# Attention sums: GpSimd adds all four key tiles into two sets of buffers, TensorE sums once per group, the output bias moves to VectorE

## The chip, the cores and the metric

The kernel runs on one core of one Trainium2 chip. A core has five engines with a queue each: TensorE (PE in the profile; PEld is its weight load), VectorE (DVE), ScalarE (ACT), GpSimd (POOL) and SyncE (SP), which issues the DMAs here. They run side by side and meet at semaphores only. The metric is device time in microseconds (us) of one execution; lower is better.

## The reference, cut to what matters

Four layers run one after another over x (4 batches of 512 tokens, 512 channels): a scan layer, a quantized feed-forward layer, an attention layer, and a last quantized projection. The change is in the attention layer:

```python
q = q.reshape(B, N, H, Dh)            # H = 16 heads of Dh = 32; N = M = 512
attn = softmax(einsum('bnhd,bmhd->bhnm', q, k) * scale, axis=-1)
o = einsum('bhnm,bmhd->bnhd', attn, v).reshape(B, N, C)
out = _qdq(o) @ _qdq(wp).T + bp
```

The result is added to x with a factor tanh(g). The bias bp, times that factor, may be added to x at any time before that; the kernel does it row by row during the attention.

## The kernel before, in words

**Groups and slots.** The attention is 16 groups: 4 batches times 4 sets of 4 heads (`HG` = 4). A group is 16 slots: slot 4t + j handles key tile t (128 keys) and head j. TensorE's `attend` writes out what each slot issues, in this order: the row matmuls of the next group (`rows`, L1161, whose maxima VectorE takes), the slot's score matmul (`scores`, L1180: 128 keys by 512 queries), then what the slot has besides. ScalarE turns each score tile into weights with an exponential (L936) and stores it in one of eight buffers `PR`. There are two PSUM banks for scores, so the score of slot s waits for the exponential of slot s - 2. Once a key tile is through, `weigh` (L1190, four matmuls of f32, eight records) multiplies the weights with the values.

**The maxima and their transfer.** The softmax needs each query's maximum before the scores begin. The row matmuls of group n + 1 run in the slots of group n (`ROWS` says how many in each; three PSUM banks take turns, so a row matmul waits for the reduction three before it). VectorE reduces each one (`maxima`, L1641). After slot 9 TensorE turns the maxima (`c_turn`, L1169); ScalarE casts them to f16 behind the exponential of slot 10 (`c_out`, L909); VectorE makes the remainder in its slot 12 (`c_low`, L1649); SyncE sends both to the operand of the next group's scores (L447, two DMAs). The first score of the next group waits for them (`c_in`).

**The sums.** The softmax's denominator is a sum of the weights over all keys. For key tiles 0, 1 and 2 GpSimd adds the weights, one buffer `ACC[j]` per head (L663, eight adds a group). TensorE then sums over the partitions with a matrix of ones, into PSUM bank 7: in slot 2 of the following group the weights of tile 3 (`sum_last`, L1209), in slot 3 the `ACC` buffers (`sum_weights`, L1199). ScalarE copies the sums out of bank 7 (`sums_out`, L921) behind the exponential of slot 5. TensorE turns the sums in slot 6 (`sum_turn`, L1227, into bank 4) and the outputs in slot 7 (`o_turn`, L1217, into bank 7, so it waits for that copy). VectorE inverts the sums in slot 8 (L1655) and normalizes the outputs in slot 9 (L1661). After a group's adds GpSimd adds the bias to one row block of x (L666).

**What sets the order.** Every engine's order is written out by hand, slot by slot; an engine takes its instructions strictly in that order and waits at each for its semaphores.

The functions that the diff touches, with what calls them:

Of the kernel before, what the change touches and what calls it, by code (L numbers as in the profile page):

```python
# [5 lines left out]
F32 = mybir.dt.float32  # L6
# [54 lines left out]
def flamingo_kernel(nc, x, ctx_2048, g_xattn, g_ffn, w, u, w1, w2, w3, wq, bq, wkv, bkv, wp, bp, gamma, wl, out):  # L61
    stack = ExitStack()
    with stack:
# [124 lines left out]
        ACC = [part(SEQ, F32) for _ in range(HG)]  # L188
# [321 lines left out]
        def _(pool):  # L510
# [142 lines left out]
            def add_weights(b, first, last):  # L653
                for g in range(DB):
                    n = b * DB + g
                    for t in (1, 2):
                        for j in range(HG):
                            pool.wait_ge(exp_done, n * 16 + HG * t + j + 1)
                            if t == 1:
                                up_to(pool, sum_ps, n)  # L660
                            else:
                                pool.wait_ge(acc_done, n * 8 + j + 1)
                            nc.gpsimd.tensor_tensor(ACC[j], PR[j] if t == 1 else ACC[j], PR[(HG * t + j) % 8],  # L663
                                                    ALU.add).then_inc(acc_done, 1)
                    rows = X[:, bass.ds(n, 1), :].rearrange("p a d -> p (a d)")
                    nc.gpsimd.tensor_tensor(rows, rows, bp_all[:, :], ALU.add).then_inc(x_biased, 1)  # L666
# [22 lines left out]
        def _(act):  # L689
# [233 lines left out]
            def attend(b, first, last):  # L923
                for g in range(DB):
                    n = b * DB + g
                    opening, closing = first and g == 0, last and g == DB - 1
                    for t in range(TB):

                        up_to(act, pv_tile, n * TB + t - 1)
                        for j in range(HG):  # L930
                            if t == 1:
                                up_to(act, sum_ps, n)
                            else:
                                up_to(act, acc_done, n * 8 + (j - 3 if t == 0 else j + 1))
# [5 lines left out]
                            if (t, j) == (1, 1) and not opening:  # L940
                                sums_out(*preceding(b, g))
# [54 lines left out]
        def _(pe):  # L996
# [167 lines left out]
            def c_turn(b, g):  # L1164
                n = b * DB + g
                pe.wait_ge(row_max, n * 16 + 16)
                up_to(pe, den_ready, n - 1)
# [26 lines left out]
            def sum_weights(b, g):  # L1194

                n = b * DB + g
                pe.wait_ge(acc_done, n * 8 + 8)
                for j in range(HG):
                    last_ = mm(bank[7][DH * j:DH * j + DH, :], ones[:, 0:DH], ACC[j], start=False, stop=True)  # L1199
# [20 lines left out]
            def sum_turn(b, g, final=False):  # L1220
# [3 lines left out]
                pe.wait_ge(ct_ready, n + (1 if final else 2))  # L1224
                pe.wait_ge(ct_low, n + (1 if final else 2))
# [7 lines left out]
            def attend(b, first, last):  # L1233
                for g in range(DB):
                    opening, closing = first and g == 0, last and g == DB - 1
                    ahead = coming(b, g)
                    for slot in range(16):
# [8 lines left out]
                        if slot == 2 and not opening:  # L1246
                            sum_last(*preceding(b, g))
                        if slot == 3 and not opening:
                            sum_weights(*preceding(b, g))
                        if slot == 6 and not opening:  # L1250
                            sum_turn(*preceding(b, g))
                        if slot == 7 and not opening:
                            o_turn(*preceding(b, g))
                        if slot == 9 and not closing:
                            c_turn(*following(b, g))

# [554 lines left out]
```

## Time and profile before

| What | Value |
|---|---|
| Time, median of 3 runs | 958.81 us (956.99 to 959.91) |
| The profiled execution's own time | 957.3 us |
| Its span, first to last instruction | 955.6 us |
| Busy over the span | PE 815.5 (85%), DVE 750.0 (78%), ACT 576.9 (60%), POOL 486.9 (51%) us |
| Chain that ended last, by engine | PE 37%, DVE 22%, issue 7%, ACT 6%, SP's queue 4%, DMA 3% |
| Attention, first score to first projection | about 586 to 856 us |

The page's shares run over four layers with different limits, so they don't say what the attention waits for; the rows below are taken from its stretch. A row gives the start (us from the span's start), the length, the engine, the line, what it writes and reads, how many instructions are merged, and in brackets the idle time of the engine before it with what ended it. Engines overlap neighbouring instructions by some hundredths of a us.

### The profile page before, as it was taken

The page shows a single profiled execution, that of the slowest core. Times are in us where ns is not written, and L with a number is a line of the kernel's source. Part 1 is how long each engine was busy: PE and PEld are TensorE (multiplying, and loading weights), DVE is VectorE, ACT ScalarE, POOL GpSimd, SP SyncE. Part 2 cuts the span into 40 slices and gives each one's busy share as a digit, 9 for nine tenths or more (in the row PEclk, how much of TensorE's full clock was granted, in tenths as well). Part 3 has the DMA queues.
Part 4 walks back from the last instruction along what each step waited for, and adds up shares of the span by engine and source line. Part 5 has one row for each costly group of instructions (what it writes and reads, how often), then busy time and mean ns, then how long its engine had stood idle before and what let it go on. Part 6 is the DMA issues. An engine that isn't in the chain of part 4 may idle for free.

```text
span 955.6 us, 14530 instructions
## 1 busy us (share of the span) xinstructions
PE 815.5 (85%) x4373; PEld 352.5 (37%) x4373; DVE 750.0 (78%) x1494; ACT 576.9 (60%) x974; POOL 486.9 (51%) x560
## 2 busy tenths in 40 slices
PE   2899987789999999899999967799999999974754
PEld 2545443334344444444444432223232232212321
DVE  4699998878899899899888757577777777634885
ACT  3588886543566565666555544466666666655762
POOL 2956663223334344354443344476757575764761
PEclk9999998899999999999999987999999999997886
DMA  8668965533343342344333242212121221000111
GB/s 282 221 188 216 224 204 151 147 90 67 69 108 56 72 105 56 72 62 78 67 64 59 45 103 63 78 48 82 51 82 54 77 58 46 1 1 0 44 66 67
DMA packets 172392, 86.51 MB, mean 91 GB/s; under 512 B 124048, under 2 KB 156960, under 8 KB 172320
## 3 DMA queue, kind: packets, MB, share of 16 engines
q1 hardware_dynamic: 172320, 85.64, 36.0%
q8 instruction: 34, 0.56, 0.3%
q14 instruction: 38, 0.31, 0.1%
HBM read 37.76 MB, written 12.58 MB: 53 GB/s over the span
## 4 chain that ended last, share of the span: by engine, by line
PE 37%; DVE 22%; issue 7%; ACT 6%; SPq 4%; DMA 3%; POOL 0%; ACTq 0%; DVEq 0%
PE bank L1098 10%; PE bank L1190 5%; PE bank L1161 5%; PE bank L1110 5%; PE bank L1180 4%; DMA A<-B 3%; DVE bank L1515 3%; DVE gsm L1517 3%; DVE B L1526 2%; SPq L438 2%; DVE B L1520 2%; PE bank L1307 2%; ACT bank L806 2%; PE bank L1199 2%; PE bank L1209 2%
## 5 line engine op out<-in xcount | busy, mean ns | idle before, releaser
L1098 PE MATMUL bank<-A,B 128*128 128x512 f16 x1024 | 232.4, 380 | 13.2 <-DVE B L1526 13.1
L1641 DVE TENSOR_REDUCE B<-bank 128x1 f32<-128x512 f32 x256 | 167.9, 683 | 72.8 <-PE bank L1161 72.8
L936 ACT ACTIVATE A<-bank 128x512 f32<-128x512 f32 x256 | 143.9, 593 | 105.6 <-PE bank L1180 102.1
L594 POOL TENSOR_TENSOR B<-B 128x512 f16<-128x512 f32 x64 | 75.8, 1184 | 216.9 <-DVE B L1526 132.2
L1098 PEld LDWEIGHTS bank<-A,B 128*128 128x128 f16 x1024 | 99.1, 98 | 138.5 <-DVE B L1526 16.4
L663 POOL TENSOR_TENSOR B<-A 128x512 f32<-128x512 f32 x64 | 79.3, 1269 | 94.0 <-ACT A L936 94.0
L1110 PE MATMUL bank<-A,B 128*128 128x512 f16 x512 | 120.7, 379 | 0.0
L806 ACT ACTIVATE bank<-B 128x512 f32<-128x512 f32 x64 | 38.5, 602 | 130.4 <-DVE B L1520 130.4
L1180 PE MATMUL bank<-A 98*128 98x512 f16 x256 | 93.8, 387 | 20.9 <-ACT A L936 10.5
L1161 PE MATMUL bank<-A 96*128 96x512 f16 x256 | 96.2, 400 | 10.5 <-DMA A<-B 5.0
L663 POOL TENSOR_TENSOR B<-B,A 128x512 f32<-128x512 f32 x64 | 79.0, 1264 | 0.6 <-ACT A L936 0.6
L1190 PE MATMUL bank<-A,B 128*32 128x512 f32 x512 | 69.1, 612 | 1.0 <-ACT A L936 1.0
L1110 PEld LDWEIGHTS bank<-A,B 128*128 128x128 f16 x512 | 49.5, 98 | 54.3 <-DMA B<-B 0.3
L1073 PE MATMUL bank<-B 128*128 128x512 f16 x192 | 48.2, 405 | 17.1 <-DVE B L1411 17.0
L1515 DVE SCALAR_TENSOR_TENSOR bank<-bank,ffs,B 128x512 f32<-128x512 f32 x64 | 48.3, 755 | 11.8 <-PE bank L1098 10.6
L1526 DVE SCALAR_TENSOR_TENSOR B<-bank,gsm 128x512 f32<-128x512 f32 x64 | 44.2, 691 | 16.1 <-ACT bank L806 14.0
L1161 PEld LDWEIGHTS bank<-A 96*128 96x128 f16 x256 | 23.1, 99 | 86.1 <-DVE B L1641 68.0
L801 ACT ACTIVATE B<-bank,ffs 128x512 f32<-128x512 f32 x64 | 43.2, 675 | 17.4 <-PE bank L1098 17.1
L549 POOL TENSOR_SCALAR B<-X,mv,rs 128x128 f32<-128x128 f32 x64 | 49.8, 792 | 0.4
L1180 PEld LDWEIGHTS bank<-A 98*128 98x128 f16 x256 | 24.9, 99 | 66.8 <-ACT A L936 36.6
L1517 DVE TENSOR_REDUCE gsm<-bank 128x8 f32<-128x512 f32 x64 | 44.3, 692 | 2.2
L1520 DVE TENSOR_TENSOR B<-bank,gsm 128x512 f32<-128x512 f32 x64 | 44.2, 691 | 2.2
(215 smaller groups left out, 1465.4 us busy)
## 6 DMA issues: line engine op xcount, KB each, us to landing
B<-in_L_ffn_w_dram SPq DMA_DIRECT2D x48, 256.0 KB, 3.4
A<-k_parts SPq DMA_DIRECT2D x48, 128.0 KB, 2.6
A<-B SPq DMA_DIRECT2D x192, 32.0 KB, 1.9
X<-in_x_dram SPq DMA_DIRECT2D x4, 1024.0 KB, 9.2
B<-in_ctx_dram SPq DMA_DIRECT2D x16, 256.0 KB, 5.0
k_parts<-B SPq DMA_DIRECT2D x16, 256.0 KB, 4.4
v_rows<-B SPq DMA_DIRECT2D x16, 256.0 KB, 2.4
B<-v_rows SPq DMA_DIRECT2D x16, 256.0 KB, 3.1
```

Of the source, the lines that this page charges most:

```text
L594: nc.gpsimd.tensor_tensor(HLb[j][:, 1, :], Db[j % 2], HLb[j][:, 0, :], ALU.subtract).then_inc(lo_done, 1)
L663: nc.gpsimd.tensor_tensor(ACC[j], PR[j] if t == 1 else ACC[j], PR[(HG * t + j) % 8], ALU.add).then_inc(acc_done, 1)
L936: nc.scalar.activation(PR[(HG * t + j) % 8], bank[2 + j % 2][:, :], ACT.Exp, scale=SCALE).then_inc(exp_done, 1)
L1098: last = mm(bank[2 * n + q][:, :], XQT[a][:, m, :], wt[:, m % DB, j * 512:j * 512 + 512], start=(m == 0), stop=(m == 2 * DB - 1))
L1110: last = mm(bank[5 + q][:, :], HT[j][:, m, :], W3T[:, DB * j + m % DB, :], start=(j == 0 and m == 0), stop=(j == FC - 1 and m == 2 * DB - 1))
L1161: mm(bank[ROW_BANKS[r % 3]][:, :], QS[0:96, HG * g + j, t * P:t * P + P], KS[0:96, HG * g + j, :], start=True, stop=True).then_inc(row_ps, 1)
L1180: mm(bank[2 + j % 2][:, :], KS[0:98, HG * g + j, t * P:t * P + P], QS[0:98, HG * g + j, :], start=True, stop=True).then_inc(st_ps, 1)
L1190: last_ = mm(bank[6][DH * j:DH * j + DH, :], VB[:, t, (HG * g + j) * DH:(HG * g + j + 1) * DH], PR[(HG * t + j) % 8], start=(t == 0), stop ...
L1515: stt(H, H, C2, SAb[q], ALU.mult, ALU.mult).then_inc(h_done, 1)
L1517: link(reduce(gsm[:, 0, :], grouped(H), AX.X, ALU.max, apply_absolute_value=True))
L1520: tt(grouped(Tb[q]), grouped(H), spread(2), ALU.mult).then_inc(t_done, 1)
L1641: reduce(NMX[g % 2][:, t, j:j + 1], bank[ROW_BANKS[r % 3]][:, :], AX.X, ALU.max, negate=True).then_inc(row_max, 1)
```

## The change

GpSimd now also adds key tile 3, twelve adds a group, and writes them into two sets of `ACC` buffers in turn; the second set lies in buffers of the layer before. TensorE's separate sum of tile 3 is gone except after the last group, whose order stays as it was. `sum_weights` stands in slot 5 (was slot 3) and starts the PSUM sum itself. `sums_out` stands behind the exponential of slot 7 (was 5), `o_turn` in slot 8 (was 7), `sum_turn` in slot 13 (was 6), and VectorE's inversion and normalization in slots 14 and 15 (were 8 and 9). The bias row is added by VectorE in slot 10. The waits are renumbered to match.

```diff
-        ACC = [part(SEQ, F32) for _ in range(HG)]
+        ACC = [[part(SEQ, F32) for _ in range(HG)],
+               [a.bitcast(F32).rearrange("p n t -> p (n t)") for a in XQT] + [a.rearrange("p k t -> p (k t)") for a in (QF, QB)]]
...
             def add_weights(b, first, last):
                 for g in range(DB):
-                    n = b * DB + g
-                    for t in (1, 2):
+                    n, acc = b * DB + g, ACC[g % 2]
+                    for t in range(1, TB - 1 if last and g == DB - 1 else TB):
                         for j in range(HG):
                             pool.wait_ge(exp_done, n * 16 + HG * t + j + 1)
                             if t == 1:
-                                up_to(pool, sum_ps, n)
+                                up_to(pool, sum_ps, n - 1)
                             else:
-                                pool.wait_ge(acc_done, n * 8 + j + 1)
-                            nc.gpsimd.tensor_tensor(ACC[j], PR[j] if t == 1 else ACC[j], PR[(HG * t + j) % 8],
+                                pool.wait_ge(acc_done, n * 12 + HG * (t - 2) + j + 1)
+                            nc.gpsimd.tensor_tensor(acc[j], PR[j] if t == 1 else acc[j], PR[(HG * t + j) % 8],
                                                     ALU.add).then_inc(acc_done, 1)
-                    rows = X[:, bass.ds(n, 1), :].rearrange("p a d -> p (a d)")
-                    nc.gpsimd.tensor_tensor(rows, rows, bp_all[:, :], ALU.add).then_inc(x_biased, 1)
...
-                            if t == 1:
-                                up_to(act, sum_ps, n)
-                            else:
-                                up_to(act, acc_done, n * 8 + (j - 3 if t == 0 else j + 1))
+                            up_to(act, acc_done, n * 12 + (j - 7, j - 3, j + 1, j + 1)[t])
...
-                            if (t, j) == (1, 1) and not opening:
+                            if (t, j) == (1, 3) and not opening:
                                 sums_out(*preceding(b, g))
...
             def c_turn(b, g):
...
-                up_to(pe, den_ready, n - 1)
+                up_to(pe, den_ready, n - 2)
...
-            def sum_weights(b, g):
+            def sum_weights(b, g, final=False):
...
-                pe.wait_ge(acc_done, n * 8 + 8)
+                pe.wait_ge(acc_done, n * 12 + (8 if final else 12))
+                if not final:
+                    up_to(pe, sm_ready, n)
+                    up_to(pe, o_norm, n)
                 for j in range(HG):
-                    last_ = mm(bank[7][DH * j:DH * j + DH, :], ones[:, 0:DH], ACC[j], start=False, stop=True)
+                    last_ = mm(bank[7][DH * j:DH * j + DH, :], ones[:, 0:DH], ACC[g % 2][j], start=not final, stop=True)
...
-            def sum_turn(b, g, final=False):
+            def sum_turn(b, g):
...
-                pe.wait_ge(ct_ready, n + (1 if final else 2))
-                pe.wait_ge(ct_low, n + (1 if final else 2))
+                pe.wait_ge(ct_ready, min(n + 3, DB * BATCH))
+                pe.wait_ge(ct_low, min(n + 3, DB * BATCH))
...
-                        if slot == 2 and not opening:
-                            sum_last(*preceding(b, g))
-                        if slot == 3 and not opening:
+                        if slot == 5 and not opening:
                             sum_weights(*preceding(b, g))
-                        if slot == 6 and not opening:
-                            sum_turn(*preceding(b, g))
-                        if slot == 7 and not opening:
+                        if slot == 8 and not opening:
                             o_turn(*preceding(b, g))
                         if slot == 9 and not closing:
                             c_turn(*following(b, g))
+                        if slot == 13 and not opening:
+                            sum_turn(*preceding(b, g))
...
-                        if slot == 8 and not opening:
-                            invert_sums(*preceding(b, g))
-                        if slot == 9 and not opening:
-                            normalize(*preceding(b, g))
+                        if slot == 10:
+                            bias_row(b * DB + g)
                         if slot == 12 and not closing:
                             c_low(*following(b, g))
+                        if slot == 14 and not opening:
+                            invert_sums(*preceding(b, g))
+                        if slot == 15 and not opening:
+                            normalize(*preceding(b, g))
...
+            def bias_row(i):
+
+                row_ = flat(X[:, bass.ds(i, 1), :])
+                tt(row_, row_, bp_all[:, :], ALU.add).then_inc(x_biased, 1)
```

TensorE, before, slots 2 to 6 of a group: L1209 and L1199 are the two sums, L1161 the row matmuls, L1180 the scores, L1190 `weigh`, L1227 `sum_turn`.

```order
L1209 MATMUL bank<-A,ones 32x512 x4
L1161 MATMUL bank<-A 128x512 x2
L1180 MATMUL bank<-A 128x512
L1199 MATMUL bank<-B,ones 32x512 x4
L1161 MATMUL bank<-A 128x512
L1180 MATMUL bank<-A 128x512
L1161 MATMUL bank<-A 128x512
L1180 MATMUL bank<-A 128x512
L1190 MATMUL bank<-A,B 32x512 x4
L1161 MATMUL bank<-A 128x512
L1180 MATMUL bank<-A 128x512
L1227 MATMUL bank<-id,B 128x128 x4
```

Now, slots 5 to 9: L1186 is `weigh`, L1198 the one sum, L1157 the row matmuls, L1176 the scores, L1216 `o_turn`.

```order
L1186 MATMUL bank<-A,B 32x512 x4
L1198 MATMUL bank<-B,ones 32x512 x4
L1157 MATMUL bank<-A 128x512
L1176 MATMUL bank<-A 128x512
L1157 MATMUL bank<-A 128x512
L1176 MATMUL bank<-A 128x512
L1157 MATMUL bank<-A 128x512
L1176 MATMUL bank<-A 128x512
L1216 MATMUL bank<-id,B 128x128 x4
L1157 MATMUL bank<-A 128x512
L1176 MATMUL bank<-A 128x512
```

One sum is left and stands directly behind `weigh`; `sum_turn` is no longer in this place, and `o_turn` has moved from slot 7 to slot 8.

ScalarE, before, one group from the exponential after a cast: L936 exponentials, L915 the copy of the outputs, L921 the copy of the sums (`sums_out`), L909 the cast of the maxima (`c_out`).

```order
L936 ACTIVATE A<-bank 128x512 x9
L915 COPY B<-bank 128x512
L936 ACTIVATE A<-bank 128x512 x2
L921 COPY B<-bank 128x512
L936 ACTIVATE A<-bank 128x512 x5
L909 CAST B<-bank 4x512
```

Now, with L932, L914, L920 and L908 for the same.

```order
L932 ACTIVATE A<-bank 128x512 x9
L914 COPY B<-bank 128x512
L932 ACTIVATE A<-bank 128x512 x4
L920 COPY B<-bank 128x512
L932 ACTIVATE A<-bank 128x512 x3
L908 CAST B<-bank 4x512
```

The copy of the sums stands two exponentials later.

VectorE, before, around slot 12: L1641 the maxima, L1655 the inversion, L1661 the normalization, L1649 `c_low`, L1683 a maximum over the outputs of the batch before.

```order
L1655 RECIPROCAL B<-bank 128x16
L1641 TENSOR_REDUCE B<-bank 128x1
L1661 TENSOR_TENSOR B<-bank,B 128x4x128
L1641 TENSOR_REDUCE B<-bank 128x1 x2
L1649 TENSOR_TENSOR B<-bank,B 4x512
L1641 TENSOR_REDUCE B<-bank 128x1 x2
L1683 TENSOR_REDUCE B<-B 128x1
```

Now: L1638 the maxima, L1687 the bias row, L1646 `c_low`, L1652 and L1658 inversion and normalization, L1682 the maximum over the outputs.

```order
L1638 TENSOR_REDUCE B<-bank 128x1 x13
L1687 TENSOR_TENSOR X<-X,bp_all 128x512
L1638 TENSOR_REDUCE B<-bank 128x1
L1646 TENSOR_TENSOR B<-bank,B 4x512
L1638 TENSOR_REDUCE B<-bank 128x1 x2
L1652 RECIPROCAL B<-bank 128x16
L1658 TENSOR_TENSOR B<-bank,B 128x4x128
L1682 TENSOR_REDUCE B<-B 128x1
```

Ahead of `c_low` the two reductions of slots 10 and 12 now have the bias row between them; inversion and normalization stand behind it.

## Rows read from the trace of the kernel before

**Rows 1.** Windows: length; busy (count) of PE, PEld, DVE, ACT, POOL; clock; DMA.

```profile
607.50:838.00 230.50, 215.53 (x1281) 64.88 (x1281) 166.80 (x270) 143.99 (x266) 153.34 (x125) 0.99 0.20 56
```

**Rows 2.** Timeline, PE, first scores, groups 1, 2, 14: start, us, what, [idle<-releaser].

```profile
607.51 0.39 PE L1180 MATMUL bank<-A 98*128 98x512 f16 x1 [4.27 <-DMA A<-B]
625.48 0.38 PE L1180 MATMUL bank<-A 98*128 98x512 f16 x1 [0.41 <-DMA A<-B]
822.11 0.38 PE L1180 MATMUL bank<-A 98*128 98x512 f16 x1 [0.41 <-DMA A<-B]
```

**Rows 3.** Timeline, PE, one group from its first score on.

```profile
707.40 0.39 PE L1180 MATMUL bank<-A 98*128 98x512 f16 x1 [0.37 <-DMA A<-B]
709.59 0.38 PE L1180 MATMUL bank<-A 98*128 98x512 f16 x1
709.90 1.06 PE L1209 MATMUL bank<-A,ones 128*32 128x512 f32 x8
710.90 0.61 PE L1161 MATMUL bank<-A 96*128 96x512 f16 x2
713.32 0.38 PE L1180 MATMUL bank<-A 98*128 98x512 f16 x1
714.62 0.39 PE L1161 MATMUL bank<-A 96*128 96x512 f16 x1
715.07 0.60 PE L1227 MATMUL bank<-id,B 128*128 128x128 f32 x4
715.51 0.38 PE L1161 MATMUL bank<-A 96*128 96x512 f16 x1
715.73 0.38 PE L1180 MATMUL bank<-A 98*128 98x512 f16 x1
719.00 0.59 PE L1180 MATMUL bank<-A 98*128 98x512 f16 x2
```

**Rows 4.** Timeline, DVE, ACT, SP queue: slots 10 to 13 of that group.

```profile
719.20 1.34 DVE L1641 TENSOR_REDUCE B<-bank 128x1 f32<-128x512 f32 x2 [0.34 <-PE bank L1161]
719.42 0.60 ACT L936 ACTIVATE A<-bank 128x512 f32<-128x512 f32 x1 [1.31 <-PE bank L1180]
719.91 0.56 ACT L909 CAST B<-bank 4x512 f16<-4x512 f32 x1
720.50 0.68 DVE L1649 TENSOR_TENSOR B<-bank,B 4x512 f16<-4x512 f32 x1
721.26 1.35 SPq L447 DMA_DIRECT2D A<-B  x2
```

**Rows 5.** Timeline, DVE, the two reductions of slot 3.

```profile
711.33 1.29 DVE L1641 TENSOR_REDUCE B<-bank 128x1 f32<-128x512 f32 x2 [0.46 <-PE bank L1161]
```

**Rows 6.** Timeline, ACT, an exponential and the copy behind it.

```profile
711.76 0.60 ACT L936 ACTIVATE A<-bank 128x512 f32<-128x512 f32 x1 [1.16 <-PE bank L1180]
712.25 0.58 ACT L915 COPY B<-bank 128x512 f32<-128x512 f32 x1
```

**Rows 7.** Timeline, POOL, that group: two runs of adds and the bias row.

```profile
713.97 4.96 POOL L663 TENSOR_TENSOR B<-A 128x512 f32<-128x512 f32 x4 [5.26 <-ACT A L936]
718.89 4.93 POOL L663 TENSOR_TENSOR B<-B,A 128x512 f32<-128x512 f32 x4
723.79 1.26 POOL L666 TENSOR_TENSOR X<-X,bp_all 128x512 f32 x1
```

**Rows 8.** Groups by line, DVE: a tensor_tensor with both inputs in SBUF.

```profile
L1430 DVE TENSOR_TENSOR B<-B,gsm 128x512 f32<-128x512 f32 x16 | 10.9, 683 | 0.1
```

**Rows 9.** Timeline, POOL and DVE: DVE operations that start inside a GpSimd add.

```profile
234.26 1.15 POOL L594 TENSOR_TENSOR B<-B 128x512 f16<-128x512 f32 x1 [4.58 <-ACT B L811]
234.58 1.38 DVE L1507 TENSOR_TENSOR bp_all<-bp_all,vec 128x512 f32<-128x512 f32 x1
847.16 1.30 DVE L1709 TENSOR_SCALAR B<-B 128x12 f32<-128x12 f32 x1
848.38 1.27 POOL L663 TENSOR_TENSOR B<-B,A 128x512 f32<-128x512 f32 x1
```

More of the change, by code:

```diff
@@ L1287, in _ @@
             sum_last(BATCH - 1, DB - 1)
-            sum_weights(BATCH - 1, DB - 1)
-            sum_turn(BATCH - 1, DB - 1, True)
+            sum_weights(BATCH - 1, DB - 1, True)
+            sum_turn(BATCH - 1, DB - 1)
             o_turn(BATCH - 1, DB - 1)
```

## The prediction

> **What bounds the kernel now.** I read the windows first, then the waits of the score matmuls, then one group's timeline engine by engine. The attention's steady stretch is 230.5 us long; TensorE is busy for 215.5 of it, VectorE for 166.8, GpSimd for 153.3, ScalarE for 144.0, at a granted clock of 0.99 [rows 1]. That looks like a TensorE bound, and then less TensorE work would be time won. The waits say otherwise. The first score of each group stands idle until a DMA lands: 0.41 us in group 2, 0.41 in group 14 [rows 2], 0.37 in the group that I lay out below [rows 3], and in each of the 13 groups 2 to 14 between 0.37 and 0.42. What lands is the maxima's transfer, which begins with `c_turn` after slot 9 of the group before. So a group is a loop: first score, slots 0 to 9, `c_turn`, cast, `c_low`, transfer, next first score. The whole loop sets the time, not TensorE's load, and a microsecond taken from TensorE counts only if it lies on the loop. From group 2 to group 14 it takes (822.11 - 625.48) / 12 = 16.39 us [rows 2]. I cut it at the score of slot 10: 719.00 - 707.40 = 11.60 us up to it [rows 3], and 16.39 - 11.60 = 4.79 us from it to the next first score.
>
> **From the first score to slot 10.** The two sums leave slots 2 and 3. One costs the gap from a score to the next slot's row matmul, 710.90 - 709.59 = 1.31, less the usual step of 715.73 - 715.51 = 0.22, so 1.09 us [rows 3]: -2.18 for both.
>
> Not all of it is won. Six row matmuls of slots 2 to 5 now follow each other without those pauses, and VectorE takes two reductions in 1.29 us [rows 5], about 0.65 each. With three banks the sixth waits for the third's reduction. The first still comes 1.75 us after the group's first score (709.59 less two steps of 0.22, less 707.40) and reaches VectorE 0.43 later (710.90 to 711.33) [rows 3, 5]; three reductions end 1.94 after that, at 4.12, and the score of slot 5 comes at 4.34. Without the limit it would come at 713.32 - 707.40 - 2.18 = 3.74 [rows 3]. So +0.6; at least +0.2 in any case, because that score also waits for the exponential of slot 3.
>
> The one sum left, in slot 5 behind `weigh`, costs the eight matmuls' 710.90 - 709.90 = 1.00 [rows 3]: +1.0. `sum_turn` leaves slot 6: 715.51 - 715.07 = 0.44, so -0.44 [rows 3].
>
> `o_turn` writes bank 7 and waits for ScalarE's copy out of it. That copy now stands behind the exponential of slot 7, and `o_turn` is only one slot further. The exponential starts 0.42 after its score (719.00 to 719.42) [rows 3, 4], some 0.1 later here because the one before it still runs; the copy starts 0.49 behind and takes 0.58 [rows 6]: 1.6 us after slot 7's score. TensorE is there after three steps of 0.22, 0.66. It waits 0.9 to 1.0, at the head of a queue in which slot 9 and `c_turn` stand behind it: +1.0.
>
> Sum: -2.18 + 0.6 + 1.0 - 0.44 + 1.0 = -0.02. What the dropped sum saves on the loop is spent on it again.
>
> **From slot 10 to the next first score.** VectorE reduces slot 10's row matmul from 719.20, then slot 12's, and starts `c_low` at 720.50; ScalarE's cast, which `c_low` needs, ends at 719.91 + 0.56 = 720.47 [rows 4]. VectorE has no slack there, and SyncE issues the transfer as soon as `c_low` is done, at 721.26 [rows 4]. The bias row now stands between those two reductions, so its whole time is added to the loop. What left slots 8 and 9 of VectorE gives nothing back: the reduction of slot 10 starts only once its matmul has run, in both orders.
>
> What the bias row costs: the nearest operation, a VectorE tensor_tensor of this size with both inputs in SBUF, took 683 ns, or 0.6 start to start [rows 8]. But another such one took 1.38 us: it started at 234.58 inside a GpSimd add that ran from 234.26 to 235.41, and ended 0.55 after that add [rows 9]. A second case: a VectorE operation on 12 elements took 1.30 us, to 848.46, just past the start of GpSimd's next add at 848.38 [rows 9]. So the bias row waits for the running add to end and then takes 0.55. GpSimd will be adding then: its twelve adds take 1.23 us each ((718.89 - 713.97) / 4 [rows 7]), 14.8 in all, from the exponential of slot 4 on, and slot 10 lies in the middle of them. The wait lies between 0 and 1.23. Laid out: slot 3's score at 3.1, exponential +0.42, copy +0.49 and 0.58, exponential of slot 4 0.60 [rows 4, 6], so adds from 5.2; their third is held 0.2 by slot 6's exponential; the sixth ends at 5.2 + 7.4 + 0.2 = 12.8, and the bias row comes up at 11.6 + 0.2 + 0.6 = 12.4. I take 0.4 + 0.55, rounded to 1.0; its bounds are 0.6 (no meeting) and 1.8 (a whole add).
>
> The Trainium skill (SBUF — State Buffer, "Who interferes with whom") states the same as a rule: a VectorE instruction with two SBUF inputs and a GpSimd instruction that reads SBUF exclude each other for a whole instruction. It speaks against putting the bias row into a stretch of GpSimd adds; without it the term would be 0.6, by it 0.55 plus the wait. The trace agrees (1.38 us against 683 ns).
>
> `sum_turn`, now in slot 13, adds 0.44 to TensorE's own way to the first score, which then takes 4.79 - 0.4 + 0.44 = 4.8 us against the transfer's 5.8: hidden, with 1 us to spare. Inversion and normalization in slots 14 and 15 run in that spare time.
>
> **The sum.** Per group -0.02 + 1.0 = about +0.98, so a loop of 17.4 us. It counts in 13 gaps, from group 1 to group 14: +12.7 us. The gap before group 1 hides it, since its first score waits 4.27 us for SyncE's loads ahead of the transfer [rows 2]. In the last gap there are no row matmuls left to hold the bias row back, and the order after the last group is unchanged. From the profiled execution's 957.3 that gives 970.0. That execution lies 1.5 under the median of 958.8, within the runs shown; I keep 970.
>
> **Rivals.**
>
> TensorE's queue, not the transfer, sets the start of each group (faster). For it: TensorE is 93% busy and loses 1.09 us a group, and the wait for the transfer is only 0.4. Then the loop is shorter by 2.18 - 0.6 - 1.0 + 0.44 = 1.0 with the copy in time, 13 x 1.0 = 13 us: 944. It needs both the bias row to fall into idle time of VectorE and the copy to end before slot 8; it decides from the point where the two together cost less than 0.4. Against it: the transfer's wait in all 13 groups, and a VectorE without a gap before `c_low`.
>
> No change: VectorE keeps up in slots 2 to 5 (+0.2), the copy waits 0.9, the bias row meets no add (+0.6). Per group +0.1, so 958 to 959.
>
> The bias row meets no add, the rest as forecast: +0.6 a group, 965.
>
> The bias row just misses the end of an add, or GpSimd becomes the bound. The first: +1.8 a group, 980. The second: 14.8 + 0.55 = 15.4 us of adds a group against a loop of 17.4; the sum in slot 5 would wait once an add takes 1.41 instead of 1.23, and each 0.1 us more then costs 1.2 a group: 16 us in all.
>
> **How the numbers follow.** Forecast 0.50 (963 to 977), faster by TensorE's queue 0.14, no change 0.09, no meeting 0.15, missed add or GpSimd 0.12. The forecast's bounds, all terms low or all high, are 958 and 980. The range 956 to 981 leaves out the faster rival and little above. A measurement tells about 0.3% from no change, 2.9 us. Faster 0.15, same 0.09, slower 0.76.
>
> **What would show it.** The bias rows on VectorE take over 0.7 us and end just behind a GpSimd add's end; `c_low` starts about 1 us after the cast's end; the first score waits for the DMA about 1 us, not 0.4; `o_turn` waits about 1 us for the copy of the sums; GpSimd's first adds are 17.4 us apart. It is wrong if the first score no longer waits for the DMA, if `o_turn` follows slot 8's score at once, if the sum in slot 5 waits for GpSimd, or if the clock of the stretch falls below 0.99 with TensorE's longer waits.

## The result and the profile after

| | before | after |
|---|---|---|
| Median beside each other | 959.2 us (956.99 to 959.91, 4 runs) | 973.04 us (971.52 to 973.95, 4 runs) |
| Profiled execution: span | 955.6 us | 970.5 us |
| Busy PE / DVE / ACT / POOL | 815.5 / 750.0 / 576.9 / 486.9 us | 810.9 / 759.4 / 574.0 / 549.3 us |

The ratio is 1.0145, 95% interval 1.0133 to 1.0158: slower. TensorE has less to do and GpSimd 62 us more. The same stretch as in [rows 1], a little shorter, first before and then after (length; busy time and count of PE, PEld, DVE, ACT, POOL; clock; DMA share; GB/s):

```profile
622.00:838.00 216.00, 201.35 (x1204) 60.67 (x1202) 157.71 (x256) 136.51 (x253) 147.04 (x120) 1.00 0.20 55
```

```profile
622.00:838.00 216.00, 187.60 (x1049) 57.69 (x1046) 161.98 (x262) 126.82 (x238) 191.81 (x152) 1.00 0.19 55
```

TensorE is busy for 87% of it instead of 93%, at the same clock: it lost load and gained waiting. The first scores of groups 1, 2 and 14, which answer to [rows 2]:

```profile
608.47 0.61 PE L1176 MATMUL bank<-A 98*128 98x512 f16 x1 [4.47 <-DMA A<-B]
...
627.67 0.39 PE L1176 MATMUL bank<-A 98*128 98x512 f16 x1 [0.68 <-DMA A<-B]
...
834.74 0.39 PE L1176 MATMUL bank<-A 98*128 98x512 f16 x1 [0.59 <-DMA A<-B]
```

A group now takes (834.74 - 627.67) / 12 = 17.26 us instead of 16.39, and still starts when a DMA lands. The span's 14.9 us, followed from front to back: GpSimd's first add comes 0.80 later (592.88 instead of 592.08); nothing changed ahead of it, and the attention's first row matmul is already 0.77 late (568.28 instead of 567.51). Group 1's first score is another 0.16 later. From there to group 14's first score the 13 gaps take 226.27 instead of 214.60: +11.67. The last gap and the last group take 1.7 more (below), what follows 0.55, whose cause stays open.

One group after, in rows that answer to [rows 3 to 7]. TensorE: its first score, slots 5 to 10, the next first score.

```profile
713.97 0.39 PE L1176 MATMUL bank<-A 98*128 98x512 f16 x1 [0.71 <-ACT A L932]
...
718.32 0.38 PE L1176 MATMUL bank<-A 98*128 98x512 f16 x1
...
719.62 1.07 PE L1198 MATMUL bank<-B,ones 128*32 128x512 f32 x8
720.62 0.39 PE L1157 MATMUL bank<-A 96*128 96x512 f16 x1
...
721.28 0.38 PE L1176 MATMUL bank<-A 98*128 98x512 f16 x1
...
722.97 0.63 PE L1216 MATMUL bank<-id,B 128*128 128x128 f32 x4 [0.67 <-ACT B L920]
...
725.61 0.59 PE L1176 MATMUL bank<-A 98*128 98x512 f16 x2
...
731.19 0.39 PE L1176 MATMUL bank<-A 98*128 98x512 f16 x1 [0.72 <-ACT A L932]
```

The stretches: 4.35 us to the score of slot 5 (718.32), 2.30 over `weigh` and the sum to slot 6's row matmul, 0.66 to slot 7's score (721.28), 4.33 to slot 10's (725.61), 5.58 to the next first score. The expensive one is slots 7 to 10: it took 719.00 - 715.73 = 3.27 before [rows 3]. In it, behind slot 8's score (721.91), `o_turn` (L1216) waits 0.67 for the copy of the sums.

VectorE, ScalarE, GpSimd and SyncE's queue from slot 10 on:

```profile
725.61 1.26 POOL L664 TENSOR_TENSOR B<-B,A 128x512 f32<-128x512 f32 x1
...
725.81 0.69 DVE L1638 TENSOR_REDUCE B<-bank 128x1 f32<-128x512 f32 x1 [1.27 <-PE bank L1157]
...
726.42 1.00 DVE L1687 TENSOR_TENSOR X<-X,bp_all 128x512 f32<-128x512 f32 x1
726.52 0.56 ACT L908 CAST B<-bank 4x512 f16<-4x512 f32 x1
...
726.84 1.72 POOL L664 TENSOR_TENSOR B<-B,A 128x512 f32<-128x512 f32 x1
...
727.35 0.68 DVE L1638 TENSOR_REDUCE B<-bank 128x1 f32<-128x512 f32 x1
...
727.95 0.67 DVE L1646 TENSOR_TENSOR B<-bank,B 4x512 f16<-4x512 f32 x1
...
728.69 1.35 SPq L448 DMA_DIRECT2D A<-B  x2
...
730.07 1.08 ACT L932 ACTIVATE A<-bank 128x512 f32<-128x512 f32 x2 [1.42 <-PE bank L1176]
```

The first scores at 713.97 and 731.19 are put down to ScalarE, not to the DMA. That is a coincidence of the view: the score needs the exponential of slot 14, the first of the two from 730.07, which ended at 730.67; the one that ended at 731.15, next to the score, is slot 15's. The score comes 2.50 after SyncE issued the transfer (728.69), as it did before (721.26 [rows 4] to 723.76), so here too the transfer ended the wait.

The bias row (L1687) stands between the two reductions. The cast ended at 727.08, but `c_low` (L1646) starts at 727.95: 2.34 after slot 10's score, against 720.50 - 719.00 = 1.50 before [rows 3, 4]. GpSimd's add from 725.61 ends at 726.87; the bias row ends 0.55 after it, as the operation of [rows 9] did, and the next add takes 1.72 instead of 1.26. The bias row's 16 instances have a median of 1003 ns (790 to 1564).

### The profile page after: what moved, and what is told of

Read it like the earlier page. It is cut to its first block, busy times and chain, and to the rows that moved or that the text cites. A ratio compares the mean times of both kernels' runs of the same rounds, so it can differ in the third digit from the quotient of the medians.

```text
span 970.5 us, 14453 instructions
## 1 busy us (share of the span) xinstructions
PE 810.9 (84%) x4253; PEld 351.2 (36%) x4253; DVE 759.4 (78%) x1510; ACT 574.0 (59%) x974; POOL 549.3 (57%) x604
## 4 chain that ended last, share of the span: by engine, by line
PE 36%; DVE 23%; ACT 8%; issue 8%; SPq 3%; DMA 1%; ACTq 0%; DVEq 0%
PE bank L1094 10%; PE bank L1186 6%; PE bank L1106 4%; PE bank L1157 4%; PE bank L1176 4%; DVE bank L1512 3%; DVE gsm L1514 3%; DVE B L1523 2%; DVE B L1638 2%; SPq L439 2%; ACT A L932 2%; DVE B L1517 2%; PE bank L1304 2%; ACT bank L805 2%; PE bank L1198 1%
## 5 line engine op out<-in xcount | busy, mean ns | idle before, releaser
L1094 PE MATMUL bank<-A,B 128*128 128x512 f16 x1024 | 232.9, 381 | 13.1 <-DVE B L1523 12.7
L1638 DVE TENSOR_REDUCE B<-bank 128x1 f32<-128x512 f32 x256 | 163.8, 682 | 74.3 <-PE bank L1157 73.8
L932 ACT ACTIVATE A<-bank 128x512 f32<-128x512 f32 x256 | 144.6, 598 | 122.0 <-PE bank L1176 120.6
L595 POOL TENSOR_TENSOR B<-B 128x512 f16<-128x512 f32 x64 | 75.8, 1185 | 217.0 <-DVE B L1523 128.4
L664 POOL TENSOR_TENSOR B<-B,A 128x512 f32<-128x512 f32 x124 | 159.4, 1319 | 0.6 <-ACT A L932 0.5
L1176 PE MATMUL bank<-A 98*128 98x512 f16 x256 | 94.5, 391 | 26.9 <-ACT A L932 17.6
L1157 PE MATMUL bank<-A 96*128 96x512 f16 x256 | 99.8, 406 | 11.5 <-DMA A<-B 4.9
L1186 PE MATMUL bank<-A,B 128*32 128x512 f32 x512 | 69.1, 611 | 2.4 <-ACT A L932 1.0
L800 ACT ACTIVATE B<-bank,ffs 128x512 f32<-128x512 f32 x64 | 43.3, 676 | 17.8 <-PE bank L1094 17.5
L1157 PEld LDWEIGHTS bank<-A 96*128 96x128 f16 x256 | 24.3, 100 | 75.0 <-DVE B L1638 53.3
L1176 PEld LDWEIGHTS bank<-A 98*128 98x128 f16 x256 | 25.1, 99 | 72.8 <-ACT A L932 39.2
L581 POOL TENSOR_TENSOR B<-B 128x512 f16<-128x512 f32 x16 | 18.9, 1183 | 50.7 <-ACT B L779 40.5
```

The source lines that it names most:

```text
L595: nc.gpsimd.tensor_tensor(HLb[j][:, 1, :], Db[j % 2], HLb[j][:, 0, :], ALU.subtract).then_inc(lo_done, 1)
L664: nc.gpsimd.tensor_tensor(acc[j], PR[j] if t == 1 else acc[j], PR[(HG * t + j) % 8], ALU.add).then_inc(acc_done, 1)
L932: nc.scalar.activation(PR[(HG * t + j) % 8], bank[2 + j % 2][:, :], ACT.Exp, scale=SCALE).then_inc(exp_done, 1)
L1094: last = mm(bank[2 * n + q][:, :], XQT[a][:, m, :], wt[:, m % DB, j * 512:j * 512 + 512], start=(m == 0), stop=(m == 2 * DB - 1))
L1157: mm(bank[ROW_BANKS[r % 3]][:, :], QS[0:96, HG * g + j, t * P:t * P + P], KS[0:96, HG * g + j, :], start=True, stop=True).then_inc(row_ps, 1)
L1176: mm(bank[2 + j % 2][:, :], KS[0:98, HG * g + j, t * P:t * P + P], QS[0:98, HG * g + j, :], start=True, stop=True).then_inc(st_ps, 1)
```

## Experiments

Ratios are against the kernel before on the same chip. "A group" is the mean distance of GpSimd's first adds from group 1 to group 14: 17.26 us by the first scores above for the changed kernel.

**The bias row alone**: the kernel before, with only the bias row moved.

```diff
 # GpSimd, after a group's adds
-                    nc.gpsimd.tensor_tensor(rows, rows, bp_all[:, :], ALU.add).then_inc(x_biased, 1)
 # VectorE
+                        if slot == 10:
+                            bias_row(b * DB + g)
```

> The kernel before with one part of the change alone: the bias row moves from GpSimd to slot 10 of VectorE, all else as before. Theory (the loop over the maxima's transfer sets the time, and the bias row stands in it): each bias row takes about 1.0 us, 0.6 and a wait for GpSimd's running add; c_low and the transfer come 0.85 us later, the first score's wait for the DMA grows from 0.4 to about 1.2 us, groups are 17.2 us apart instead of 16.4; 13 groups give +11 us, about 970 against 959. Rival (TensorE's queue is what the change lengthens, the sum and o_turn's wait): the bias row is hidden, 959 to 960. Second rival (the bias row counts but meets no GpSimd add): +0.6 a group, 967.

Measured 969.0 us, 1.0098 (1.0081 to 1.0115). A group takes 17.10. The timeline of one group, TensorE and VectorE:

```profile
708.48 0.59 PE L1178 MATMUL bank<-A 98*128 98x512 f16 x2
...
709.29 0.89 DVE L1688 TENSOR_TENSOR X<-X,bp_all 128x512 f32<-128x512 f32 x1
...
710.70 0.67 DVE L1647 TENSOR_TENSOR B<-bank,B 4x512 f16<-4x512 f32 x1
...
713.94 0.39 PE L1178 MATMUL bank<-A 98*128 98x512 f16 x1 [1.09 <-DMA A<-B]
```

`c_low` starts 2.22 after slot 10's score instead of 1.50, the first score 5.46 instead of 4.79, and it waits 1.09 for the DMA. With nothing else changed this move costs +0.71 a group, 13 x 0.71 = 9.2 of the 9.6 us. The bias row is on the loop. It also holds GpSimd: the four adds from 708.37 take 5.38 here, 4.93 in [rows 7].

**One input**: the changed kernel, the bias row's tensor_tensor replaced by a reduction of the same size and place that reads one operand from SBUF. This kernel leaves the bias out.

```diff
-                tt(row_, row_, bp_all[:, :], ALU.add).then_inc(x_biased, 1)
+                reduce(st1[:, 3, 0:1], row_, AX.X, ALU.max).then_inc(x_biased, 1)
```

> The changed kernel with the bias row replaced by an operation of the same length with one input from SBUF: a VectorE reduction of the row of x to one number (the bias is left out of the output). Theory (a second SBUF input makes VectorE wait for GpSimd's running add): the operation takes 0.68 us at any moment, c_low comes 0.3 us earlier than in the changed kernel (0.61 instead of 0.93 between the starts around it), groups 16.9 instead of 17.2 us apart, 13 x 0.3 = 4 us less: 969. GpSimd's runs of adds lose their pause too: eight adds in 9.9 us instead of 10.3. Rival (1.0 us is simply what such an addition costs on VectorE, or any operation is held by GpSimd): 973.

Measured 969.14 us, 1.0107 (1.009 to 1.0124), as expected in time; the groups are 17.08 apart, not 16.9. The reduction, and GpSimd's eight adds beside the next one:

```profile
708.19 0.68 DVE L1687 TENSOR_REDUCE st<-X 128x1 f32<-128x512 f32 x1
...
723.13 9.84 POOL L664 TENSOR_TENSOR B<-B,A 128x512 f32<-128x512 f32 x8
```

In the changed kernel the same eight adds, and VectorE's normalization (L1658) among them:

```profile
724.38 10.31 POOL L664 TENSOR_TENSOR B<-B,A 128x512 f32<-128x512 f32 x8
...
730.74 0.69 DVE L1658 TENSOR_TENSOR B<-bank,B 128x512 f32<-128x512 f32 x1
```

0.68 against a median of 1.00, and 9.84 against 10.31: with two inputs in SBUF the VectorE operation waits for GpSimd's running add, and GpSimd's next add waits for it. A reduction also writes less than an addition does; but the normalization is a tensor_tensor that writes a whole 128x512 block and has one of its inputs in PSUM, and it takes 0.69 in all 16 groups. That leaves the second SBUF input. By the groups (17.08 instead of 17.26) the meeting costs 13 x 0.18 = 2.3 us, by the ratios 0.38%, 3.6 us; the prediction's rival "meets no add" lay 5 us below the forecast.

**The bias row behind `c_low`**: the changed kernel, slot 13 instead of 10.

```diff
-                        if slot == 10:
-                            bias_row(b * DB + g)
                         if slot == 12 and not closing:
                             c_low(*following(b, g))
+                        if slot == 13:
+                            bias_row(b * DB + g)
```

> The changed kernel with the bias row in slot 13 of VectorE, behind c_low instead of ahead of it. Theory: the transfer comes 0.85 us earlier than in the changed kernel, and TensorE's own way from slot 10 to the next first score, 4.86 us, becomes the longer one: 5.58 - 4.86 = 0.7 us less a group, 13 groups, 973 - 9.4 = 963.6. Rival (the bias row costs nothing where it stands): 973.

Measured 971.5 us, 1.0124 (1.0107 to 1.0141): a miss, 8 us too high. The timeline of one group from slot 10's score on:

```profile
708.72 0.59 PE L1176 MATMUL bank<-A 98*128 98x512 f16 x2
...
710.22 0.68 DVE L1646 TENSOR_TENSOR B<-bank,B 4x512 f16<-4x512 f32 x1
...
713.18 2.24 ACT L932 ACTIVATE A<-bank 128x512 f32<-128x512 f32 x4 [1.42 <-PE bank L1176]
...
713.92 0.38 PE L1176 MATMUL bank<-A 98*128 98x512 f16 x1 [0.34 <-ACT A L932]
715.05 4.86 DVE L1638 TENSOR_REDUCE B<-bank 128x1 f32<-128x512 f32 x8
```

`c_low` is back at 1.50 after slot 10's score, so the bias row is off that path. But the first score comes 5.20 after slot 10's, not 4.86: it now waits for the exponential of slot 14 (713.18 to 713.78), which frees its score bank. With `sum_turn` in slot 13 that exponential is nearly as late as the DMA was. (The kernel with one input gains no more, 17.08: there, too, that exponential ends no more than 0.2 before the transfer.) The reductions behind the bias row start later and then run without a gap, and the score of slot 5 comes 718.40 - 713.92 = 4.48 after the first, not 4.35. A group takes 17.07. The theory that all of the bias row's 0.8 us comes back once it leaves `c_low`'s path fell: a second wait lay 0.4 behind it.

**`o_turn` in slot 11**: the changed kernel, nothing else moved.

```diff
-                        if slot == 8 and not opening:
-                            o_turn(*preceding(b, g))
                         if slot == 9 and not closing:
                             c_turn(*following(b, g))
+                        if slot == 11 and not opening:
+                            o_turn(*preceding(b, g))
```

> The changed kernel with o_turn in slot 11 of TensorE, after c_turn, instead of slot 8. Theory: o_turn no longer waits for the copy of the sums (0.67 us of idle, 0.19 of a late score before it), and its own 0.44 leaves the part of the loop before c_turn: 1.1 us less there; after slot 10 it is hidden, since TensorE's own way grows to 5.3 us against the transfer's 5.6. Groups 16.1 us apart, 973 - 14 = 959. Rival (waits of TensorE do not count, since the first score waits for the transfer anyway): 973.

Measured 955.49 us, 0.996 (0.9948 to 0.9973), where 959 was expected: 17.5 us less than the changed kernel, by this one move. A group takes 16.05. TensorE in one group, its first score, the scores of slots 7 and 10, and `o_turn`:

```profile
707.52 0.39 PE L1176 MATMUL bank<-A 98*128 98x512 f16 x1 [0.75 <-DMA A<-B]
...
714.83 0.38 PE L1176 MATMUL bank<-A 98*128 98x512 f16 x1
...
717.92 0.59 PE L1176 MATMUL bank<-A 98*128 98x512 f16 x2
...
718.35 0.60 PE L1216 MATMUL bank<-id,B 128*128 128x128 f32 x4
```

From slot 7's to slot 10's score 717.92 - 714.83 = 3.09, not 4.33: 1.24 of the loop. `o_turn` costs the loop its wait of 0.67 and its own matmuls; behind slot 10's score it waits for nothing and lies in time that the DMA takes anyway.

**Both moves.**

> Both moves together: bias row in slot 13, o_turn in slot 11. Theory: 10.55 us from the first score to slot 10, then TensorE's own way of 5.3 us, no wait for the DMA any more: 15.85 us a group, 973 - 17.6 = 955.5, a little faster than before. If the two gains were independent, -9.4 and -14 would give 949.6; the theory says that the second is partly hidden by TensorE's own way. Rival (GpSimd's twelve adds bound the group): groups no shorter than 15.4 to 16 us and the one sum in slot 5 waits for GpSimd, 957 or more.

Measured 951.64 us, 0.9919 (0.9903 to 0.9936); expected 955.5. A group takes 15.83. The bias move gains 0.22 a group here and 17.26 - 17.07 = 0.19 above; `o_turn`'s gains 17.07 - 15.83 = 1.24 here and 17.26 - 16.05 = 1.21 alone. The two add up.

**Then the cast and `c_low` earlier** (from "both moves": the cast behind slot 9's exponential, `c_low` in slot 11).

```diff
-                            if (t, j) == (2, 2) and not closing:
+                            if (t, j) == (2, 1) and not closing:
                                 c_out(*following(b, g))
...
-                        if slot == 12 and not closing:
+                        if slot == 11 and not closing:
                             c_low(*following(b, g))
```

> The kernel with both moves (bias row in slot 13, o_turn in slot 11), and the cast of the maxima one exponential earlier on ScalarE (behind slot 9), c_low in slot 11 of VectorE, ahead of slot 12's reduction. Theory: c_low and the transfer come 1.0 us earlier; the first score then waits only for the exponential of slot 14 and TensorE's own way: 5.1 us from slot 10 instead of 5.4, so 15.5 us a group instead of 15.8, 13 x 0.3 = 4 us less: 948. No wait for the DMA at the first score is left. Rival (GpSimd's adds, 14.8 us and 0.5 for the bias row, already bound the group): 951 to 952, and the sum in slot 5 waits for GpSimd. Second rival (the cast holds up the exponentials behind it and so the scores): 952 or more.

Measured 952.09 us, 0.9926 (0.9909 to 0.9942), where 948 was expected: no gain. A group takes 15.70. **One row matmul more in slot 1, one less in slot 3**, added to that (`ROWS` begins 1, 2, 2, 1 instead of 1, 1, 2, 2):

> The same as the kernel with the early cast, and one row matmul of the next group moved from slot 3 to slot 1 (the third of slots 0 to 5). Theory (VectorE's reductions, one every 0.6 us, hold up the scores of slots 3 to 5): the score of slot 5 comes 0.2 us earlier, 13 x 0.2 = 2.5 us less than with the early cast alone: 945 to 946, unless GpSimd's adds bound the group by then (then 947 to 948). Rival (those reductions hold up nothing): no difference.

Measured 953.3 us, 0.9939 (0.9923 to 0.9956), where 945 to 948 was expected: again none; a group takes 15.66. With the earlier cast the first score no longer waits for the transfer, in 12 of the 13 groups 2 to 14: it comes 4.84 after slot 10's instead of 5.20, behind the exponential of slot 14. But slot 5's score then comes 4.81 after the first (719.57 to 724.38) instead of 4.49 in "both moves" (719.75 to 724.24). VectorE in the kernel with the earlier cast:

```profile
717.33 1.70 DVE L1687 TENSOR_TENSOR X<-X,bp_all 128x512 f32<-128x512 f32 x1
...
721.03 4.86 DVE L1638 TENSOR_REDUCE B<-bank 128x1 f32<-128x512 f32 x8
```

The bias row in slot 13 takes 1.70 here. The eight reductions behind it start 1.46 after the group's first score and run without a gap, and the row matmuls wait for them (0.21 at 722.96); a row matmul moved forward gains nothing, since its reduction comes no earlier. So VectorE's reductions are now the wait ahead of slot 5's score. GpSimd is not the bound, although the time lies where that rival put it (951 to 952): it idles for 0.4 us of a group, and the sum starts 0.62 after its last add (709.36 to 709.98). In the last group, where there are no row matmuls, TensorE does wait for it at the sum:

```profile
836.17 1.94 PE L1198 MATMUL bank<-B,ones 128*32 128x512 f32 x8 [1.29 <-POOL B L664]
```

**The last group relieved**: TensorE sums key tile 3 of the last group but one, as it does for the last; GpSimd adds eight tiles there, not twelve. Once from "both moves", once from the earlier cast.

```diff
-                    for t in range(1, TB - 1 if last and g == DB - 1 else TB):
+                    for t in range(1, TB - 1 if last and g >= DB - 2 else TB):
...
-                        if slot == 5 and not opening:
-                            sum_weights(*preceding(b, g))
+                        if slot == 2 and closing:
+                            sum_last(*preceding(b, g))
+                        if slot == (3 if closing else 5) and not opening:
+                            sum_weights(*preceding(b, g), closing)
```

> The kernel with both moves (bias row in slot 13, o_turn in slot 11), and the last but one group's key tile 3 summed by TensorE (slots 2 and 3 of the last group, as before the change) instead of GpSimd: eight adds there. Theory (GpSimd carries four adds too many into the last group, where nothing else is slow): the sum no longer waits 1.05 us for GpSimd, the last group's adds start with its own exponential of slot 4, and the attention ends 1.5 us earlier: 950.1 against 951.6. Rival (the last group's end is set by ScalarE's exponentials alone): 951.6, the end of the attention no earlier.

> The kernel with the early cast, and the same change of the last but one group. Theory: what the early cast won in the steady groups was lost at the end, where the sum waited 1.29 us for GpSimd, the granted clock fell to half for some 10 us and the last group took 3 us longer; without that wait the clock stays up and the time is 952.1 - 1.3 - 2.5 = 948.3. Rival (the clock falls there for want of row matmuls, whoever sums): 951.

The first: 953.21 us, 0.9938 (0.9917 to 0.9959), where 950.1 was expected, not told apart from "both moves" by its interval. From GpSimd's first add of group 14 to the last `weigh` it takes 24.72 instead of 25.42, so the wait is gone; but the profiled execution's attention began with GpSimd's first add at 595.70 instead of 591.93, where the kernels do not differ. Inconclusive in time. The second: 950.56 us, 0.9915 (0.9895 to 0.9935), where 948.3 was expected, and from that add to the last `weigh` 843.85 - 819.43 = 24.42 instead of 848.42 - 820.06 = 28.36. A window of the last group, earlier cast and then relieved:

```profile
836.00:842.00 6.00, 5.51 (x20) 0.74 (x20) 0.00 (x0) 2.56 (x5) 5.15 (x6) 0.50 0.00 0
```

```profile
836.00:842.00 6.00, 4.71 (x28) 1.63 (x29) 0.00 (x0) 4.47 (x9) 6.00 (x6) 1.00 0.01 3
```

While TensorE waits for GpSimd in the earlier-cast kernel, the granted clock falls to 0.50, the lower level (1.2 GHz), and the matmuls take twice as long (the sum above: 1.94 instead of 1.07). That profiled execution was the slowest of its four, so 28.36 overstates what the relief is worth in the median; the medians, by their ratios, differ by 0.1% only, within the intervals.

**And the bias row in slot 9**, ahead of the reduction that waits for slot 10's row matmul, added to the second of these.

```diff
-                        if slot == 13:
-                            bias_row(b * DB + g)
+                        if slot == 9:
+                            bias_row(b * DB + g)
                         if slot == 11 and not closing:
                             c_low(*following(b, g))
```

> As the one before, and the bias row in slot 9 of VectorE instead of slot 13. Theory (in slot 13 it just misses an add's end, takes 1.7 us, and pushes VectorE's reductions of the next group's first slots, so that the score of slot 5 comes 0.25 us late; in slot 9 VectorE has 1.0 us of idle time and the early cast has left 0.8 us of slack to the transfer): 0.25 us a group less, 15.45 us, 3 us in all: 945 to 946. GpSimd's adds, 14.8 and 0.5, are the floor at 15.3 to 15.4. Rival (in slot 9 the bias row delays slot 10's reduction and with it c_low and the transfer): the first score waits for the DMA again, 948 to 951.

Measured 948.25 us (947.37 to 948.88), 0.9889 (0.9868 to 0.9911), where 945 to 946 was expected: the fastest of all, faster than both kernels. A group takes 15.45. VectorE and GpSimd in one group:

```profile
709.11 2.50 POOL L665 TENSOR_TENSOR B<-A 128x512 f32<-128x512 f32 x2
711.77 2.50 POOL L665 TENSOR_TENSOR B<-A 128x512 f32<-128x512 f32 x2 [0.17 <-ACT A L936]
713.29 1.53 DVE L1693 TENSOR_TENSOR X<-X,bp_all 128x512 f32<-128x512 f32 x1
```

The bias row takes 1.53 there, waiting for an add; VectorE would otherwise have idled before slot 10's row matmul (1.04 in the earlier-cast kernel, at 714.93), so the rest is what it can delay. Slot 5's score is back at 4.48 after the first (719.05 to 723.53), as the expectation had it. GpSimd idles 0.17 us of the 15.41 between its first adds (709.11 and 724.52). It is nearly the bound, but not yet: the sum (709.46) still starts 0.31 after its last add (709.15). The loop is 1 us under the 16.39 of before.

## Why the prediction was right

The forecast was 970.0; 973.04 came. The mechanism held, the sizes nearly, and the end of the attention was missed. That the total is so close is partly luck: the 13 gaps cost 1.0 less than forecast, and the end, priced at nothing, 1.7 more.

**First score to slot 10: -0.02 forecast, +0.04 measured** (11.64 against 11.60). Each term shows. Without the two sums, with VectorE's reductions in the way, the score of slot 5 was to come at 4.34 and comes at 4.35. The one sum costs 2.30 - (714.62 - 713.32) = 1.00 [rows 3]. `sum_turn` gives back 1.11 - 0.66 = 0.45. `o_turn` was to wait 0.9 to 1.0; it idles 0.67, slot 8's score comes 0.19 late ahead of it, and the whole stretch is 4.33 - 3.27 = 1.06 longer. "What the dropped sum saves on the loop is spent on it again" is what the `o_turn` experiment shows from the other side: out of slot 8 it gives 1.2 back. That is more than the +1.0, since `o_turn`'s own matmuls then leave this stretch too, in which they stood before as well.

**Slot 10 to the first score: +1.0 forecast, +0.8 measured** (5.58 against 4.79). The bias row meets an add 0.44 before its end and takes 0.56 more, as worked out (0.4 and 0.55); 0.93 from its start to the next reduction's. `c_low` is 0.84 later, not 0.93, since VectorE's two steps to it took 720.50 - 719.20 = 1.30 before [rows 4], with short waits in them, and take 1.21 without the bias row now. The rule of the Trainium skill (SBUF — State Buffer, "Who interferes with whom"), that such a pair excludes each other for a whole instruction, was weighed in the prediction; the trace agrees: 1.00 us with two inputs, 0.68 with one, and the exclusion holds GpSimd up too (1.72 instead of 1.26).

**`sum_turn`, "hidden, with 1 us to spare"**: hidden it is, but with 0.38 to spare: 5.58 against the 5.20 at which the first score comes with the bias row in slot 13, when the exponential of slot 14 ends last. The prediction took the first score's whole idle time of 0.4 off TensorE's own way (4.79 - 0.4). Before the change, ScalarE and TensorE around a first score:

```profile
722.98 2.30 ACT L936 ACTIVATE A<-bank 128x512 f32<-128x512 f32 x4 [0.94 <-PE bank L1180]
723.76 0.39 PE L1180 MATMUL bank<-A 98*128 98x512 f16 x1 [0.39 <-DMA A<-B]
```

The first of the four exponentials is slot 14's and ends 0.60 after its start, at 723.58. With the bias row in slot 13 the first score follows it by 0.14 (713.78 to 713.92). So before the change, too, this score could have come only 0.04 earlier without the transfer: the idle time names the wait that ended last and hides one just behind it. The forecast of 970 did not hang on that; the rival's point "less than 0.4" and the expectation for the bias row in slot 13 did.

**The 13 gaps**: +12.7 forecast, +11.67 measured.

**What failed: the last gap and the last group, priced at nothing.** The last gap, from group 14's first score to the last group's, takes 16.43 instead of 15.93; the last group, from its first score to its last `weigh`, 15.23 instead of 14.01: 1.7 together. "The order after the last group is unchanged" is true, but within the last group the order is new, and there is no transfer behind which `sum_turn` could hide. TensorE after, then before:

```profile
851.17 0.79 PE L1176 MATMUL bank<-A 98*128 98x512 f16 x2 [0.62 <-ACT A L932]
...
855.08 1.07 PE L1186 MATMUL bank<-A,B 128*32 128x512 f32 x8 [0.18 <-ACT B L914]
856.11 1.07 PE L1198 MATMUL bank<-B,ones 128*32 128x512 f32 x8
...
859.30 0.63 PE L1216 MATMUL bank<-id,B 128*128 128x128 f32 x4 [0.67 <-ACT B L920]
...
866.40 1.07 PE L1186 MATMUL bank<-A,B 128*32 128x512 f32 x8 [1.02 <-ACT A L932]
```

```profile
838.04 0.67 PE L1180 MATMUL bank<-A 98*128 98x512 f16 x2 [0.74 <-DMA A<-B]
...
852.05 1.07 PE L1190 MATMUL bank<-A,B 128*32 128x512 f32 x8 [1.02 <-ACT A L936]
```

The last group's first score now waits for the exponential of slot 14, no longer for the DMA, and that exponential stands behind `sum_turn`: 5.10 after slot 10's score instead of 4.73. From slot 10's score to the last `weigh` the last group takes 5.32 instead of 4.70 (from 861.08 and from 847.35), with `sum_turn` in it again. Up to slot 10's score it takes 9.91 instead of 9.31, with `o_turn`'s wait of 0.67 in it (L1216). No run takes these parts from one another.

GpSimd has little to do with it. It carries group 14's adds into the last group, and the sum (856.11) starts as the last of them ends (856.05). But `weigh` ahead of it started at 855.08, and in other groups the sum follows `weigh` by 0.86, so this wait is worth 0.17. In the kernel with one input the adds end earlier and the sum waits for nothing:

```profile
852.53 1.07 PE L1186 MATMUL bank<-A,B 128*32 128x512 f32 x8 [0.18 <-ACT B L914]
853.38 1.07 PE L1198 MATMUL bank<-B,ones 128*32 128x512 f32 x8
```

Its last gap and last group still take 31.56 together, against 31.66 in the changed kernel and 29.94 before. "The sum in slot 5 waits for GpSimd" was named as what would prove the forecast wrong in every group; it came true in one, for 0.17 us.

**The 0.8 us at the start** is not the change's: the profiles of these kernels begin the attention's adds between 591.93 and 595.70, and up to there their code is the same. One execution's span carries that much.

The rivals: TensorE's queue does not set the start of a group in the changed kernel (the loop grew although its load fell), but its own way, over the exponential of slot 14, lies only 0.38 behind the transfer. No change (958 to 959) and the bias row without a meeting (965) lie below every measured time. GpSimd as the bound came in no run: between the first and the last group no sum and no exponential waited for it, in the changed kernel or in those with the later moves.

## What to carry to other kernels

Work taken from the busiest engine is won only if it lies on the loop that sets the time; here 1 us of it was spent again by one instruction, `o_turn`, put at the head of an in-order queue 0.7 us before its input. When an operation changes engine, ask which slot of the new engine is idle, not how fast the engine is: the same bias row cost 0.7 us a group between two reductions, and the loop got 0.25 shorter when it moved ahead of a wait, though it ran 1.53 us there. A wait in a profile is the one that ended last: before you count on its removal, look for the next one behind it (here 0.04 us before the change, 0.38 after). And price the loop's last turn by itself, since what hid an instruction in the others may be missing there.

## What the runs showed of the hardware

Which of the two waits is not always the same. In the changed kernel the bias row came up 0.81 into an add, waited for its end, and held the next add. In the kernel with the bias row in slot 13 it came up 0.27 into an add and ran at once; that add took the longer (GpSimd, then VectorE):

```profile
711.16 2.06 POOL L664 TENSOR_TENSOR B<-B,A 128x512 f32<-128x512 f32 x1
...
711.43 0.67 DVE L1687 TENSOR_TENSOR X<-X,bp_all 128x512 f32<-128x512 f32 x1
```

2.06 instead of 1.26 for the add, 0.67 for the bias row. In [rows 9] an operation that started 0.32 into an add waited, so where it comes up does not settle it alone; by place in the order the bias row took 0.67 to 1.70 us in the median.

Two inputs from SBUF are not the only case. The operation on 12 elements of [rows 9] reads one, and took 1.30 us beside GpSimd's adds; in the changed kernel it comes after their end (866.61) and takes 0.17.

The granted clock fell to 0.50 within the last group of the earlier-cast kernel during TensorE's wait of 1.29 us, and in the kernel with the row matmul moved as well (0.50 in the same 836 to 842); in "both moves", whose sum waited 1.05 for GpSimd in the same place, it stayed at 1.00. No run held everything else fixed and varied that wait, so the wait as the cause is argued, not shown.
